# A recurrent mixer's ScalarE order: the first exponentials ahead of the squares, and projection reads ahead of the decay terms

## The reference, cut to what matters

```python
mixed = silu(causal_conv4(h @ W_qkv.T))          # 2048 channels: q, k (8 heads), v (16 heads)
z     = h @ W_z.T
beta  = sigmoid(h @ W_b.T)
g     = -exp(A_log) * softplus(h @ W_a.T + dt_bias)
for each position t:
    S = S * exp(g[t])
    S = S + k[t] * ((v[t] - S.k[t]) * beta[t])
    o[t] = S.q[t]
o = o * silu(z);  o = o * rsqrt(mean(o * o) + eps) * norm_weight
h = h + o @ W_out.T
```

## Time and profile before

| what | value |
|---|---|
| median of 3 runs | 3156.9 us |
| lowest and highest of them | 3155.66 and 3166.07 us |
| profiled execution, its own time | 3159.19 us |
| its span from first to last instruction | 3157.5 us |
| mean granted TensorE clock | 0.877 of full speed |
| changed stage, turns of pairs 0 to 17 | from 924 us to about 2230 us of the span |
| one turn with all four parts | about 76.6 to 80.3 us |

### The profile page before, as it was taken

How to read it: one execution, slowest core, us unless ns; L and a number is a source line. 1 busy time by engine, 2 the same in 40 slices (tenths; PEclk the granted TensorE clock), 3 DMA queues, 4 the chain that set the end, 5 groups by cost and what they waited for, 6 DMA issues and landing times. The chain is left out here.

```text
span 3157.5 us, 53822 instructions
## 1 busy us (share of the span) xinstructions
PE 2447.2 (78%) x19384; PEld 1877.8 (59%) x19384; DVE 2088.9 (66%) x5024; ACT 1247.4 (40%) x2999; POOL 809.4 (26%) x646
## 2 busy tenths in 40 slices
PE   6888886997455888888888888876543756689798
PEld 5666664886444666666667666655332644466554
DVE  4777773332338888888888888875454336687573
ACT  0434342221145666665666666643000213344132
POOL 1111100000113332233222222231287125550110
PEclk9999997998578999999999999988665887889799
DMA  5220001001212221111112211111211762110000
GB/s 138 64 67 12 12 9 52 21 24 29 87 64 51 52 52 46 49 48 49 44 48 49 51 49 48 45 44 29 74 51 24 227 198 56 47 52 10 18 24 24
DMA packets 277730, 168.94 MB, mean 54 GB/s; under 512 B 186303, under 2 KB 253702, under 8 KB 277112
## 3 DMA queue, kind: packets, MB, share of 16 engines
q1 hardware_dynamic: 251333, 140.22, 15.8%
q0 software_dynamic: 26112, 25.03, 3.0%
HBM read 99.17 MB, written 73.45 MB: 55 GB/s over the span
## 5 line engine op out<-in xcount | busy, mean ns | idle before, releaser
L1149 POOL TENSOR_TENSOR qd<-decay,qm 114x456 f32<-114x456 f32 x128 | 143.7, 1145 | 651.2 <-DVE qm L1242 499.2
L1563 PE MATMUL d_ps<-d_xT,w_qkv 128*128 128x228 f32 x1024 | 235.0, 389 | 48.3 <-DVE qmask L1357 28.9
L1563 PEld LDWEIGHTS d_ps<-d_xT,w_qkv 128*128 128x128 f32 x1024 | 215.4, 212 | 79.5 <-issue 42.0
L2216 POOL DMA_INDIRECT s_eo<-rows_y,slots_all x128 | 152.5, 1191 | 148.5 <-POOLq L87 110.5
L1210 DVE TENSOR_TENSOR elim_tmp<-ue 128x30 f32<-128x30 f32 (+14 forms) x480 | 179.3, 374 | 13.8
L463 PE MATMUL t_ps<-xT,w_qk 128*128 128x154 f32 x1024 | 150.9, 300 | 40.4 <-DVE qk L300 31.0
L1212 DVE TENSOR_TENSOR ue<-ue,elim_tmp 128x30 f32<-128x30 f32 (+14 forms) x480 | 170.4, 355 | 16.5
L1284 DVE SCALAR_TENSOR_TENSOR y_v<-raw,taps,y_v 128x228 f32<-128x228 f32 x384 | 161.2, 493 | 14.3 <-ACT y_v L1414 14.2
L463 PEld LDWEIGHTS t_ps<-xT,w_qk 128*128 128x128 f32 x1024 | 136.7, 189 | 52.0 <-DVE qk L300 38.2
L1551 PE MATMUL d_ps<-gl,after 114*114 114x456 f32 x256 | 132.7, 637 | 41.0 <-DVE sz L1297 41.0
L1376 ACT ACTIVATE decay<-d_ps,gates 114x114 f32<-114x114 f32 x512 | 133.4, 371 | 65.4 <-PE d_ps L1551 65.0
(11 more groups left out here) (337 smaller groups left out, 5656.9 us busy)
## 6 DMA issues: line engine op xcount, KB each, us to landing
rows_x<-zero_row SPq DMA_DIRECT2D x4, 2048.0 KB, 7.8
ue<-blocks_n SPq DMA_DIRECT2D x16, 512.0 KB, 4.7
blocks_u<-ue SPq DMA_DIRECT2D x16, 512.0 KB, 2.7
blocks_v<-on SPq DMA_DIRECT2D x16, 512.0 KB, 2.8
e_x<-rows_x SPq DMA_DIRECT2D x32, 256.0 KB, 4.2
e_gu<-L_ffn_w_gate_up SPq DMA_DIRECT2D x32, 256.0 KB, 4.2
rows_y<-e_y SPq DMA_DIRECT2D x32, 256.0 KB, 3.3
blocks_n<-nt SPq DMA_DIRECT2D x96, 64.0 KB
```

The costliest lines, as they stand in the source:

```text
L1149: pool.tensor_tensor(qd[p.par][s][:, hs(u), :].rearrange("p (a o b) t -> p a o b t", o=2, b=2)[:, :, o], e[o][:, :, :].rearrange("p (a b) ...
L1563: last = pe.matmul(ps[:, f % 2, (t % 2) * W:(t % 2 + 1) * W], w_qkv[:, k, t * 128:(t + 1) * 128], xT[:, k, :], start=(k == 0), stop=(k == ...
L2216: pool.indirect_dma_start(out=eo[n % 2][:, s * TOPK + k, :], out_offset=None, in_=rows_y, in_offset=bass.IndirectOffsetOnAxis(ap=slots_all ...
```

## The change

Only the order of ScalarE's instructions at the start of a turn changes. `decay_terms` of the next unit is no longer a part of `exps` but called by itself (`terms`). The exponentials of unit 0 go ahead of the two squares, and the reads of fills 0 and 1 go ahead of the decay terms of unit 1. From unit 1 on the order is what it was. No instruction is added or removed, and no wait's condition is altered.

```diff
                         if a:
                             decay_exp(p, 2 * v)
                             decay_exp(p, 2 * v + 1)
-                            if v < 3:
-                                decay_terms(p, v + 1)
-
+
+                    def terms(v):
+                        if a:
+                            decay_terms(p, v)
+
+                    exps(0)
                     if d:
                         gate_squares(done, 0)
                         gate_squares(done, 1)
-                    exps(0)
-                    raws(0, 4)
+                    raws(0, 2)
+                    terms(1)
+                    raws(2, 4)
                     exps(1)
+                    terms(2)
                     raws(4, 6)
                     if d:
                         oT_read(done, 0)
                         oT_read(done, 1)
                     exps(2)
+                    terms(3)
                     raws(6, 8)
```

## The result

| | kernel before | changed kernel |
|---|---|---|
| median of 4 runs | 3159.43 us | 3174.63 us |
| lowest to highest | 3155.66 to 3166.07 | 3168.01 to 3179.29 |
| profiled execution: time, span | 3159.19, 3157.5 | 3168.01, 3166.3 |

The ratio is 1.0048 (95% interval 1.0025 to 1.007): slower by about 15 us, outside my range of 3146 to 3166, and on the side of rival C.

What follows compares the result with a forecast made beforehand. TensorE and VectorE were taken to hand the turn to each other. The terms -3.5 - 0.5 - 1.6 - 0.8 + 5.1 gave -1.3 us, so 3155.6 us against the median of 3156.9; range 3146 to 3166.

Steps and rivals of the forecast that it cites:

- rival C: TensorE's clock falls beside `on` in nearly every turn: eight more slow products, +13.6 less 3.5, 3167 us; chance 0.12.
- Squares later, terms later: ScalarE, turn start: squares have 2.1 us of cover before `gate_mean`, unit 1's decay terms 1.3 us before TensorE's sums.
- Fill 2 without a wait: TensorE's fill 2 starts right after fill 1, no longer waiting for ScalarE's read; 0.33 us in the turn shown.
- Gain given back at `on`: TensorE reaches its wait for VectorE's `on` 0.3 to 1.3 us sooner and idles that much longer there.
- Early turns: Turns of pairs 0 and 1, where fill 2 starts sooner: gains of 3.5 and 0.5 us.
- The turn near 1520: One turn with a 2.68 us wait and slow fills 2 and 3: the clock should hold, gaining 1.6 us.
- oT_read earlier: ScalarE's reads of fills 4 and 5 end earlier, so `oT_read` starts at once: 0.1 us over 8 turns, 0.8 us.
- The clock: Longer TensorE idle time before the output turn slows the output product in three more turns, 1.7 us each: 5.1 us lost.

Runs made afterwards that it cites:

- e2: Kernel before with only the reads of fills 0 and 1 ahead of unit 1's decay terms, squares still first; 3182.39 us, 1.0053 to the kernel before.
- e8: Kernel before with reads of fills 0 and 1 ahead of the decay terms only in turns without an output part; 3160.58 us, ratio 0.9987.
- e10: The changed kernel again, word for word; 3178.74 us, 1.0038 to the kernel before.
- e3: Changed kernel plus unread TensorE products, three ahead of sample 0's output turn and one behind it; 3150.75 us, 0.9949 to the kernel before.
- e9: Changed kernel plus three unread TensorE products between the decay sums of halves 0 and 1; 3166.33 us, 1.0004 to the kernel before.
- e11: Changed kernel plus one unread TensorE product between output turn and output product only; 3164.42 us, 0.9997 to the kernel before.

## Why the prediction was wrong, step by step

- **Squares later, terms later: right.** Both were hidden. e2 has the old place of the squares and is as slow as the whole; nothing waits for them in the trace.
- **Fill 2 without a wait: right.** TensorE's weight loads waited for the reads 24.7 us over 15 times before, and 7.6 us over 6 times after. Two of the six are the early turns; in the 13 steady turns the products themselves show two waits, of 0.52 us each.
- **Gain given back at `on`: right, and the core of it.** Output turns start 15.5, 15.8 or 16.2 us into a turn in both kernels. The mean gap ahead of the output turn grew by 1.20 us. That is more than was moved: the 1.16 us that I worked with is the wait of the weight loads, and the products themselves had waited 0.86 us a turn for the reads (11.2 us in 13 turns) and now wait 0.08. The rest of the growth comes from TensorE itself, which spends less of its time ahead of the output turn at 1.2 GHz (38 us instead of 47).
- **Early turns: -3.5 - 0.5, measured -3.6** (e8: -2.8), but not reliably: in e10, the same kernel again, the stretch took 131.2 us, -0.7. The six traces with the reads ahead of the terms and the early fills as they were (the changed kernel, e2, e3, e9 to e11) have 128.3 to 131.5 us, so -0.4 to -3.6. The sum was right for one trace and too large for others.
- **The turn near 1520: -1.6, right in kind.** No turn of the changed kernel has its output turn at 17.8 us; before, one had, and in e8 one again.
- **oT_read earlier, -0.8: wrong.** In turns with a quick product the residual stands where it did: 21.64 us into the turn after an output turn at 15.5 in both kernels, 21.98 after one at 15.8. There was nothing.
- **The clock, "I estimate three turns more, 3 x 1.7 = 5.1 us": this is the step that failed**, in both factors. There were five more slow products in both traces of the changed kernel, and a slow turn is 2.3 us longer than a quick one before and 2.8 after, not 1.7. The price was read from the product alone, 5.40 against 3.71 us; with a gap of 2 us or more most of the product falls in the slow stretch and it takes 5.7 to 6.6 us in six of the ten. On average a slow product held 1.6 us over 3.71 before and 2.1 after, so 10 x 2.1 - 5 x 1.6 = 13 us, where the sum had 5.1; the old five became dearer too. What makes the rest of a slow turn's 2.3 to 2.8 us, about 0.7, I did not trace. The steady turns together measured +13.9, and with the -3.6 of the early turns the mixer up to pair 14 is 10.3 us longer, where my sum had -1.3. The medians lie further apart still (15.2 us).
- **The chances.** Rival C had the mechanism, its place and its direction, at 0.12. Its price was off as well: it took only 3.5 us of gains from the 13.6, and with all 6.4 of my own sum it stands at 3156.9 + 7.2 = 3164, inside my range. At 1.7 us each, even a slow product in every turn could not have given what was measured. Its argument "each lost turn also needs the gaps to fall badly" was the mistake: when the gap is 0.8 us, five of 13 fell badly; at 2.0 us, ten did. With idle time widened so far, the bad case is the rule.

The Trainium skill ("TensorE: Matmul & The Clock Gate", Part 1) was weighed in the prediction as a rule by which gaps under 2 us would leave the clock alone. The traces do not agree: before, the product behind gaps of 0.75 and 0.94 us took 5.40 us at a clock that had fallen, and after, with 2.15 and 0.86 us idle and the output turn of 1.01 us between them, the clock stood at 0.50. That the moment is not tied to the kernel agrees: equal gaps gave unequal products before, and the same changed kernel had its 10 slow ones partly in other turns the second time.

## What to carry to other kernels

Here an engine's wait that went away off the path came back as idle time at the next thing it waited for. On TensorE, look at what follows that place: the product right behind the lengthened gap got the slow clock in 10 turns of 13, and that product was on the path. If such a gap can't be used, fill it: four products a turn that nothing reads turned +0.48% into -0.51%, and e3 is the version that beats both kernels. Real work in the gap won less here (0.998), and lost in the kernel before (1.0047), because its own inputs were not there in time; that must be read on the engine that frees its bank.

## What the runs showed of the hardware that was not expected

The granted clock changed between its two levels on gaps of about 2 and 0.9 us around 1 us of work, far from a long idle stretch. The count of slow products was the same in two executions of the changed kernel (10 of 13) while which turns they were in changed: the turns near 1048 and 1526 of the first were quick and slow, the same two of the second slow and quick.
